# An eight-expert stage on one core: the rows of all four batches fetched by indirect DMA instead of two

## The reference, cut to what matters

```python
capacity = int(512 * 2.0 / 8) + 1                       # 129
scores = softmax(einsum('bsd,ed->bse', x, router_w))
gate_vals, sel_idx = top_k(swapaxes(scores, 1, 2), capacity)
tokens = x[b_idx, sel_idx]                              # (4, 8, 129, 128)
h = gelu(einsum('becd,edh->bech', tokens, w1) + b1)     # hidden 512
y = einsum('bech,ehd->becd', h, w2) + b2
out = zeros_like(x).at[b_idx, sel_idx].add(y * gate_vals[..., None])
```

## Time and profile before

| | us |
|---|---|
| median of 3 runs | 775.03 |
| lowest and highest | 768.9 and 779.73 |
| the profiled execution | 776.74 |
| its span, first to last instruction | 774.8 |
| PE busy | 642.5 (83%) |
| DVE busy | 589.9 (76%) |
| ACT busy | 496.1 (64%) |
| POOL busy | 456.3 (59%) |
| mean granted TensorE clock | 0.894 |

### The profile page before, as it was taken

How to read it: one execution, slowest core, us unless ns; L and a number is a source line. 1 busy time by engine, 2 the same in 40 slices (tenths; PEclk the granted TensorE clock), 3 DMA queues, 4 the chain that set the end, 5 groups by cost and what they waited for, 6 DMA issues and landing times. The chain is left out here.

```text
span 774.8 us, 8846 instructions
## 1 busy us (share of the span) xinstructions
PE 642.5 (83%) x2913; PEld 394.4 (51%) x2913; DVE 589.9 (76%) x799; ACT 496.1 (64%) x931; POOL 456.3 (59%) x260
## 2 busy tenths in 40 slices
PE   4946677796699999999986699999999962399993
PEld 2344456432445565555532445565555551389992
DVE  6794986554799999999765799999999858844521
ACT  3553334468799988889668799988989543033321
POOL 1236653100388989879700398989879715058866
PEclk9885877679699999999999699999999965599998
DMA  5000000000223222323100223223322181013333
GB/s 194 0 3 1 0 1 0 1 2 7 80 81 104 89 95 85 106 91 93 48 3 9 78 84 102 88 98 85 104 93 93 46 300 54 1 22 42 39 32 27
DMA packets 30780, 48.05 MB, mean 62 GB/s; under 512 B 3736, under 2 KB 12328, under 8 KB 30224
## 3 DMA queue, kind: packets, MB, share of 16 engines
q1 hardware_dynamic: 25600, 44.45, 18.0%
q0 software_dynamic: 5136, 3.05, 3.6%
HBM read 42.98 MB, written 4.49 MB: 61 GB/s over the span
## 5 line engine op out<-in xcount | busy, mean ns | idle before, releaser
L468 POOL TENSOR_TENSOR hc_all<-hs_all,c_row 128x1024 f32<-128x1024 f32 x88 | 207.3, 2368 | 133.2 <-DVE hs_all L1644 129.9
L1130 PE MATMUL ps<-hc_all,ident 128*128 128x512 f32 x512 | 239.1, 598 | 3.8 <-POOL hc_all L468 2.7
L1644 DVE TENSOR_TENSOR_SCAN hs_all<-da,ps 128x1024 f32<-128x1024 f32 x88 | 198.2, 2271 | 17.1 <-ACT da L794 9.6
L794 ACT ACTIVATE da<-big,a_neg 128x511 f32<-128x511 f32 x256 | 169.2, 709 | 30.5 <-DVE w_ffn L1644 27.6
L1130 PEld LDWEIGHTS ps<-hc_all,ident 128*128 128x128 f32 x512 | 90.2, 192 | 87.5 <-issue 74.2
L468 POOL TENSOR_TENSOR hc_all<-w_ffn,c_row 128x1024 f32<-128x1024 f32 x40 | 94.6, 2365 | 31.7 <-DVE w_ffn L1644 31.7
L1644 DVE TENSOR_TENSOR_SCAN w_ffn<-da,ps 128x1024 f32<-128x1024 f32 x40 | 91.4, 2284 | 3.8 <-ACT da L794 0.9
L1150 PE MATMUL ps<-ident,dbu 128*128 128x128 f32 x464 | 61.6, 276 | 10.5 <-ACT dbu L769 5.0
L1150 PEld LDWEIGHTS ps<-ident,dbu 128*128 128x128 f32 x464 | 53.2, 142 | 27.3 <-issue 16.3
L532 POOL DMA_INDIRECT out<-hc_all,hs_all x32 | 52.2, 1632 | 12.0 <-issue 9.2
L1635 DVE TENSOR_TENSOR ps<-big,ps 128x1024 f32<-128x1024 f32 x42 | 50.8, 1210 | 0.6 <-PE ps L1159 0.4
(11 more groups left out here) (281 smaller groups left out, 1029.9 us busy)
## 6 DMA issues: line engine op xcount, KB each, us to landing
c_row<-c_rows SPq DMA_DIRECT2D x128, 256.0 KB, 3.1
tmpA<-w_in SPq DMA_DIRECT2D x2, 1024.0 KB, 7.1
tmpB<-w_in SPq DMA_DIRECT2D x2, 1024.0 KB, 9.8
x_tok<-x_in SPq DMA_DIRECT2D x2, 512.0 KB, 5.5
out<-x_tok SPq DMA_DIRECT2D x1, 1024.0 KB, 11.4
xm_rows<-xn SPq DMA_DIRECT2D x1, 1024.0 KB, 5.0
w_mod<-w_mod_in SPq DMA_DIRECT2D x2, 384.0 KB, 6.3
w_ffn<-w_ffn_in SPq DMA_DIRECT2D x1, 560.0 KB, 7.6
```

Of the source, the lines that this page charges most:

```text
L468: nc.gpsimd.tensor_tensor(hc[:, n % 4, :, :], hs3[HS_BUF[n]].rearrange("p (i s) -> p i s", i=IC), c_row[:, n % 4, :].unsqueeze(1).to_broad ...
L794: ins = nc.scalar.activation(da[:, n % 2, i, 1:S], dtT[:, b, i, 1:S], ACT.Exp, scale=a_neg[:, l, i, n:n + 1])
L1130: mm = nc.tensor.matmul(ps[:, YS + i, :], ident[:], hc[:, n % 4, i, :], start=(n == 0), stop=(n == NS - 1))
L1644: v.tensor_tensor_scan(hs3[HS_BUF[n]], decay, pair.rearrange("p i s -> p (i s)"), 0.0, ALU.mult, ALU.add).then_inc(c_scan, 1)
```

## The change

Experts 1 to 7 fetch all four batches by DMA; the 12 matmuls each for batches 0 and 1 are no longer issued, and four transposes stand in place of two. The buffer grows from 2 to 4 blocks of 128 columns per half, inside the same tensor hc_all, and the wait ahead of the transposes counts 16 x 4 = 64 per fetched expert instead of 32. Expert 0, the picks, the lists, the outputs and the writes stay as they are; POOL's loop over BY_DMA in gather_rows now issues four DMAs per expert instead of two.

```diff
@@ -264,8 +264,8 @@
-        BY_DMA = [2, 3]
-        x_rows_dma = hc_all[:, 2816:2816 + 4 * D].rearrange("p (k j d) -> p k j d", k=2, j=2)
+        BY_DMA = [0, 1, 2, 3]
+        x_rows_dma = hc_all[:, 2816:2816 + 2 * B * D].rearrange("p (k j d) -> p k j d", k=2, j=B)
@@ -1278,7 +1278,7 @@
                 if e:
-                    pe.wait_ge(ld_rows[e % 2], 32 * ((e + 1) // 2 if e % 2 else e // 2))
+                    pe.wait_ge(ld_rows[e % 2], 16 * B * ((e + 1) // 2 if e % 2 else e // 2))
                     for j, b in enumerate(BY_DMA):
                         mm = nc.tensor.transpose(ps[:, XG, b * P:(b + 1) * P], x_rows_dma[:, e % 2, j, :], ident[:])
```

## The result

The changed kernel takes 793.82 us in the median of 4 runs (791.63 to 796.49), the kernel before in the same runs 775.69: a ratio of 1.023, with a 95% interval of 1.0185 to 1.0276. It is slower by some 18 us, and the forecast was 792.0.

The account below looks back on a forecast made before the run. POOL's queue, full at 10.2 us per expert and level with PE, was taken as the bound. Span 774.8 + 16.7 = 791.5 us, 791.7 on the median, stated as 792.0 us, 2.2% slower; range 786 to 799.

Parts of the forecast that it names:

- Steps 1 to 3: POOL, fetches of experts 1 and 2: two more each, so expert 0's first write begins 4.87 us late.
- 4: expert 0's writes: POOL, expert 0's four writes: keep their time, the single long one of 3.21 us taken as happening once.
- Step 5: POOL, fetches of experts 3 to 7: two more each at 1.295 us, 12.95 us in all.
- Step 6: Wait before L524, the last slots' write: the writes' landing, 3.3 us from start, ends it; gives back 1.1 us.
- Step 7: From L524, the eight last writes and the end: 22.4 us as before.
- Rival 1: Expert loop: POOL absorbs the fetches and PE's saving shows; 768.4 us, 0.9% faster; chance 0.06.
- Rival 2: Expert loop: PE's clock falls in the new waits and PE becomes the bound; dear form 798 us, chance 0.14.
- the mild case: Expert loop: a clock fall of 3.5 us costs PE 1.75, less than its 3.7 of slack: nothing.
- Rival 3: POOL: fetches in a row cheaper than between writes, sums end the wait before L524; 789.5 to 790; chance 0.10.
- The prediction's own signs: POOL's loop: right if successive experts' fetches stand 12.7 to 12.9 apart; wrong if fetches leave 0.94 to 1.01 or POOL waits.

Follow-up runs that it names:

- PE's half: Kernel before with two fetches, four transposes, no gather matmuls for experts 1 to 7: 780.66 us, ratio 1.0073; with picks one step earlier too: 774.57 us, ratio 1.0001.
- POOL's half: Changed kernel with all four batches fetched, but PE still making batches 0 and 1 with the 24 matmuls: 793.96 us, ratio 1.0281.

## Why the prediction was right

The direction, the cause and the size of the time held: POOL's queue was full at 10.2 us, every added fetch became time, and PE's saving was worth nothing. But that the median came out within 2 us of the forecast is in part luck. The stage grew by 22.3 us between the two profiles (19.6 to 23.1 over all pairs of the two each), where the sum had 16.7. The medians differ by only 18.1, and the early or late end of the part ahead, some 4 us, is the one difference seen that could make up the rest; that it did was not shown. Step by step, from the two profiled executions, each against the start of expert 1's fetch (680.38 before, 676.30 after):

| step of the walk | predicted | measured |
|---|---|---|
| 1 to 3: fetches of experts 1 and 2, to expert 0's first write | 4.87 | 4.25 |
| 4: expert 0's writes | 0 | -0.51 |
| 5: fetches of experts 3 to 7 | 12.95 | 18.00 |
| writes of experts 1 to 5 | 0 | -0.23 |
| 6: the wait before L524 gives back | 1.1 | 0.37 |
| 7: from L524 to the end | 0 | 1.24 |
| sum | 16.7 | 22.4 |

- *Step 5 was mis-sized.* I took the price of a fetch from its neighbours in the loop, 1.295. But these neighbours never met the picks: in the kernel before, the picks run beside the first write. With the queue longer, they fall on the fetches, and ten more fetches cost 18.0 instead of 12.95, which is 1.80 each and above the 1.62 that the prediction gave as the most. With the picks early in the changed kernel these fetches measure 0.94 to 1.07, and the period 12.6 to 12.95, about as predicted. The trace of before had two signs of it, which both started in a stretch of picks: the write of 3.21 us, which I took "as happening once", and the first fetch of 1.32, which I took for the dearest unloaded one.
- *Steps 1 to 3.* The fourth fetch of a row landed 2.48 after its start, not 3.16 as the second had the earlier trace rows. That is 0.68 less, and accounts for the difference. (The row of two transposes reads 0.22 and not 0.23; nothing hangs on it.)
- *Step 6.* L524, released by the landing, started 4.1 after the last write, where I had 3.3; the mechanism, a landing in place of the sums, was the right one. That L524 stands at 769.47, near the forecast 769, is luck: the whole stage began 4 us earlier.
- *Step 7.* Behind the last write's start stand 7.0 us instead of 5.8 (see below).
- *Rival 1* (POOL absorbs the fetches) fell with the two runs of PE's half. *Rival 2:* the clock did fall, to a mean of 0.77 to 0.88 in the three periods of the windows above, and in the run of POOL's half it fell less (0.87 and 1.00), without a difference in time: it was hidden, as the mild case had it. *Rival 3* was half right: third and fourth fetches of a row take 0.94, but the picks took more than that gave.
- *The prediction's own signs.* Fetches four in a row "clearly other than 0.94 to 1.01" were to show it wrong, and in four of five rows of the loop they were, up to 3.11; successive experts stood 13.6 to 14.8 apart and not 12.7 to 12.9. The gaps of 0.30, the place of PE's wait and the absence of waits on POOL were as it said. So the bound was right and its price wrong.

The Trainium skill, "DMA: Bandwidth & Descriptors", section "Anatomy of one DMA — SWDGE (gpsimd) path", which the prediction cites for many descriptors before their cost shows, is not borne out for these indirect DMAs: with the picks out of the way a fetch held POOL for mostly 1.24 to 1.31 us, gap included (at most 1.48).

## What to carry to other kernels

POOL's instructions followed each other at a constant gap of 0.30, and the queue was full although it showed 82% busy in the loop. Add up one period with the gaps before giving such a queue more work. Taking work off one of two level engines buys nothing, and it moves the phases: here it put DVE's picks beside GpSimd's fetches and cost 0.7%. When a row is used as the price of more of the same, look at what runs beside it there, and what will run beside the new ones.

## What the hardware showed that I had not expected

- A fetch that takes 0.94 to 1.01 us on POOL took up to 3.2 beside two-input bf16 DVE operations of 0.68 us each, though not always (1.15 and 0.94 in the four runs with the picks early), and 0.94 to 1.10 beside one-input ones of 0.25 us.
- The program's end grows with the number of fetches, though the last writes are the same: from the start of the last write to the end of the span it is 5.7 to 5.8 us with two fetches per expert (five profiles), 6.4 with three (one), and 6.9 to 7.0 with four (six). That is 0.6 us for seven fetches. What it consists of was not tried.
- The part ahead of the stage ends at one of two times some 4 us apart, in the same kernel too. The cause is open.
